# State carries by sync-engine transfers, four diagonal states, a root by logarithm and exponential with a Heron step, and a third norm row on GpSimd, in a fused scan-and-quantized-matmul kernel

## The reference

```python
def _s6(x, A_log, D, x_proj_w, dt_proj_w, dt_proj_b):      # x is layernorm(x)
    A = -jnp.exp(A_log)                                    # (512, 16)
    xp = jnp.einsum('bld,ed->ble', x, x_proj_w)            # 96 columns: rank 64, B 16, C 16
    delta = softplus(xp[..., :64] @ dt_proj_w.T + dt_proj_b)
    deltaA = exp(delta * A); deltaB_u = delta * B * x      # both (b, l, 512, 16)
    h = deltaA_t * h + deltaB_u_t; y_t = sum_n h_n * C_tn  # scan over 2048 steps
    return y + x * D
def _xla_quantized_matmul(x2d, weight_q, weight_scale):    # x2d is layernorm of the first layer's output
    amax = jnp.max(jnp.abs(x2d), axis=-1, keepdims=True)
    x_scale = jnp.maximum(amax, 1e-6) / 127.0
    x_q = clip(round(x2d / x_scale), -128, 127)            # int8
    return (x_q @ weight_q.T) * x_scale * weight_scale     # + bias, + x
```

## Time and profile before

| | |
|---|---|
| median of 3 runs | 2841.26 us (2841.11 to 2842.9) |
| the profiled execution's own time | 2839.73 us |
| its span, first to last instruction | 2837.9 us |
| busy: TensorE (PE) | 2798.8 us, 99% |
| busy: GpSimd (POOL) | 2758.2 us, 97% |
| busy: VectorE (DVE) | 2714.1 us, 96% |
| busy: ScalarE (ACT) | 2708.3 us, 95% |
| granted TensorE clock, mean | 0.998 |
| bytes moved | 321.24 MB, mean 113 GB/s |

### The profile page before, as it was taken

The page is one execution under the profiler, slowest core; times in us unless marked ns, Lnnn a source line. Parts: engine busy times, 40 slices in busy tenths (PEclk is TensorE's granted clock), DMA queues, the critical chain, the costliest instruction groups (busy, mean ns, idle before and its releaser), DMA issues.

```text
span 2837.9 us, 59945 instructions
## 1 busy us (share of the span) xinstructions
PE 2798.8 (99%) x22838; PEld 2544.0 (90%) x22900; DVE 2714.1 (96%) x2765; ACT 2708.3 (95%) x4990; POOL 2758.2 (97%) x1072
## 2 busy tenths in 40 slices
PE   8999999999999999999999999999999999999997
PEld 6889899899999898998998998989989989989886
DVE  6999999999999999999999999999999999999995
ACT  7999999999999999999999999999999999999993
POOL 4899999999999999999999999999999999999997
PEclk9999999999999999999999999999999999999999
DMA  5234434444434444344444344443444443444434
GB/s 188 94 106 101 129 103 127 115 115 96 127 109 115 114 100 129 102 125 118 113 98 126 110 114 116 100 129 101 125 119 113 98 127 109 114 116 98 116 91 82
DMA packets 198369, 321.24 MB, mean 113 GB/s; under 512 B 93057, under 2 KB 93057, under 8 KB 181698
## 3 DMA queue, kind: packets, MB, share of 16 engines
q1 hardware_dynamic: 164242, 250.29, 26.6%
q0 software_dynamic: 33840, 67.11, 15.4%
HBM read 212.70 MB, written 104.66 MB: 112 GB/s over the span
## 4 chain that ended last, share of the span: by engine, by line
PE 45%; POOL 35%; issue 18%; DMA 1%; DVE 0%; SPq 0%; POOLq 0%; ACT 0%; DVEq 0%
POOL A L482 27%; PE Y L707 15%; PE PB L685 10%; PE PB L682 10%; POOL C L499 3%; PE PM L747 2%; PE PM L766 2%; PE Y L703 2%; PE PM L810 2%; POOL C L491 2%; PE PM L795 1%; POOL RO L453 1%; PE PM L775 1%; PE PM L737 1%; POOL XN L438 1%
## 5 line engine op out<-in xcount | busy, mean ns | idle before, releaser
L482 POOL TENSOR_TENSOR A<-A,CB 128x2048 f32<-128x2048 f32 x511 | 2361.3, 4754 | 13.1 <-ACT CAR L545 10.9
L836 DVE TENSOR_TENSOR_SCAN A<-A,CAR,PB 128x512 f32<-128x512 f32 x1536 | 1845.8, 1264 | 40.9 <-PE PB L682 26.9
L538 ACT ACTIVATE A<-DEL,an 128x512 f32<-128x512 f32 x2048 | 1354.3, 713 | 0.4
L707 PE MATMUL Y<-idf,A 128*128 128x128 f32 x8192 | 1123.5, 273 | 1.9 <-POOL A L482 1.9
L707 PEld LDWEIGHTS Y<-idf,A 128*128 128x128 f32 x8192 | 945.5, 141 | 71.5 <-issue 41.9
L560 ACT ACTIVATE DB<-XN,BC 128x512 f32<-128x512 f32 x1408 | 966.5, 713 | 4.4 <-DVE XN L866 4.4
L685 PE MATMUL PB<-idf,DB 128*128 128x128 f32 x5632 | 801.5, 273 | 10.2 <-ACT DB L560 5.7
L685 PEld LDWEIGHTS PB<-idf,DB 128*128 128x128 f32 x5632 | 652.1, 141 | 49.0 <-issue 28.8
L682 PEld LDWEIGHTS PB<-DG,XN 128*128 128x128 f32 x5120 | 612.0, 192 | 61.3 <-issue 49.7
L682 PE MATMUL PB<-DG,XN 128*128 128x128 f32 x5120 | 638.4, 276 | 3.9 <-DVE A L836 3.3
L836 DVE TENSOR_TENSOR_SCAN A<-A,PB 128x512 f32<-128x512 f32 x512 | 589.4, 1203 | 30.6 <-PE PB L682 20.0
(11 more groups left out here) (88 smaller groups left out, 1661.1 us busy)
## 6 DMA issues: line engine op xcount, KB each, us to landing
CB<-c_rows SPq DMA_DIRECT2D x128, 1024.0 KB, 6.3
DG<-b_diag SPq DMA_DIRECT2D x160, 256.0 KB, 2.8
out<-bib SPq DMA_DIRECT2D x32, 1024.0 KB, 5.2
out<-X POOLq DMA_DIRECT2D x32, 1024.0 KB, 9.7
X<-in_x SPq DMA_DIRECT2D x31, 1024.0 KB, 5.5
out<-C POOLq DMA_DIRECT2D x31, 1024.0 KB, 8.9
b_diag<-DG SPq DMA_DIRECT2D x2, 1280.0 KB, 10.9
b_diag<-BC SPq DMA_DIRECT2D x160, 2.0 KB, 5.5
```

What stands on the lines that cost most here:

```text
L482: gp.tensor_tensor(A[s % NA][:, :, :], A[s % NA][:, :, :], CB[:, s % (4 * NG), :].unsqueeze(1).broadcast_to([128, KB, L]), ALU.mult).then_ ...
L538: act.activation(A[s % NA][:, g, :], DEL[k % 2][:, g, :], ACT.Exp, scale=an[:, g, n:n + 1])\
L707: i = pe.matmul(Y[j][:, g * 128:(g + 1) * 128], A[s % NA][:, g, j * 128:(j + 1) * 128], idf[:, :], is_transpose=True, start=False, stop=(n ...
L836: dve.tensor_tensor_scan(A[s % NA][:, g, :], A[s % NA][:, g, :], PB[(4 * s + g) % NPB][:, :], init, ALU.mult, ALU.add).then_inc(s_scan, 1)
```

## The change

- `carry` moves from ScalarE to the sync engine: a transfer from A's last column to CAR, with a semaphore of its own for each state (`s_car[n]`). `times_c` and the next chunk's `scan` wait for it.
- Diagonal states are 2, 6, 10 and 14; the other twelve are scaled (`act_b` has 48 instructions per chunk where it had 44).
- NXP = 3: one norm row of a chunk on ScalarE, three on GpSimd.
- The power on GpSimd is replaced. ScalarE (`root`) takes the logarithm of the largest square v, and the exponential of half of it, r. VectorE (`inv`) takes 1/r. GpSimd (`ascale`) forms v (1/r) + r, which is twice the root after one Heron step; the constants in the scale are doubled to match.
- All three tables of places are new.

```diff
-    DIAG = (2, 5, 8, 11, 14)
-    SCALED = tuple(n for n in range(NS) if n not in DIAG)
+    ROWS = {2: 4, 6: 4, 10: 4, 14: 4}
+    DIAG = tuple(ROWS)
+    SCALED = tuple(n for n in range(NS) if ROWS.get(n, 0) < T)
+    BYACT = tuple((n, j) for n in SCALED for j in range(ROWS.get(n, 0), T))
-    NXP = 2
+    NXP = 3
-        s_car = sem("s_car")
+        s_car = [sem(f"s_car{n}") for n in range(NS)]
+        def carried(k):
+            return 16 * (k + 1 - (k + 1) // CPB)
@@ sync engine
+            def carry(k, n):
+                s = NS * k + n
+                if k % CPB != CPB - 1:
+                    sp.wait_ge(s_scan, 4 * (s + 1))
+                    sp.dma_start(CAR[:, n, :], A[s % NA][:, :, L - 1], allow_slow_non_contiguous=True)\
+                      .then_inc(s_car[n], 16)
@@ GpSimd, ascale
-                gp.wait_ge(s_am, p + (T if p == END else 1))
-                gp.tensor_tensor(RO[:, 1, :], PW[:, 1, :], halves[:, :], ALU.pow).then_inc(s_as, 1)
+                gp.wait_ge(s_ir, p + 1)
+                gp.tensor_tensor(PW[:, 3, :], PW[:, 1, :], RO[:, 3, :], ALU.mult).then_inc(s_qu, 1)
+                gp.wait_ge(s_qu, p + 1)
+                gp.tensor_tensor(RO[:, 1, :], PW[:, 3, :], RO[:, 2, :], ALU.add).then_inc(s_as, 1)
...
-                gp.tensor_scalar(AM[:, 1, :], AM[:, 0, :], 1e-6 * D, 1.0 / (127.0 * D), ALU.max, ALU.mult).then_inc(s_zm, 1)
+                gp.tensor_scalar(AM[:, 1, :], AM[:, 0, :], 2e-6 * D, 1.0 / (254.0 * D), ALU.max, ALU.mult).then_inc(s_zm, 1)
@@ GpSimd, times_c
-                    gp.wait_ge(s_car, car_done(s))
+                    gp.wait_ge(s_car[n], carried(k))
@@ ScalarE
-            def carry(k, n):
-                s = NS * k + n
-                if k % CPB != CPB - 1:
-                    act.wait_ge(s_scan, 4 * (s + 1))
-                    act.activation(CAR[:, n, :], A[s % NA][:, :, L - 1], ACT.Copy).then_inc(s_car, 1)
+            def root(p):
+                act.wait_ge(s_am, p + (T if p == END else 1))
+                if p >= 1:
+                    act.wait_ge(s_as, p)
+                act.activation(PW[:, 2, :], PW[:, 1, :], ACT.Ln, bias=eps[:, 1:2]).then_inc(s_la, 1)
+                act.wait_ge(s_la, p + 1)
+                act.activation(RO[:, 2, :], PW[:, 2, :], ACT.Exp, scale=0.5).then_inc(s_ro, 1)
@@ VectorE
-                        dve.wait_ge(s_car, car_done(s - NS))
+                        dve.wait_ge(s_car[n], carried(k - 1))
+            def inv(p):
+                dve.wait_ge(s_ro, p + 1)
+                if p >= 1:
+                    dve.wait_ge(s_qu, p)
+                dve.reciprocal(RO[:, 3, :], RO[:, 2, :]).then_inc(s_ir, 1)
```

More of the change, by code:

```diff
@@ L7 @@
 PLACES = {
[L8 to L18, removed]
@@ L27 @@
[L27 to L39, removed]
@@ L40 @@
[L40 to L47, removed]
@@ new lines @@
+        885, 894, 905, 928, 933),
+        "delta": (-328, -284, -235, -221),
+        "dl_t": (-309, -291, -263, -215),
+        "du": (-241, -233, -135, -119),
+        "gather": (1216, 1240, 1295, 1314),
+        "idle": (247, 276, 296, 679),
+        "inv": (1630,),
+        "last_q": (1001, 1470, 1786, 1918),
+        "load": (-1797,),
+        "load_c": (17, 237, 390, 949),
+        "load_g": (127, 354, 507, 642),
+        "log0": (-1390,),
+        "put_bias": (-2127,),
+        "q_mm": (2047, 2065, 2123, 2170),
@@ new lines @@
+        "q_t": (1836, 1871, 1973, 2015),
+        "qt_out": (1892, 1950, 2000, 2052),
+        "root": (1618,),
+        "rstd0": (-1110,),
+        "scale_a": (2122, 2154, 2179, 2296),
+        "scale_out": (1189, 1260, 1438, 1757),
+        "scale_p": (2225, 2238, 2250, 2286),
+        "scales": (1647,),
+        "scan": (-1, 2, 28, 41, 62, 72, 74, 75, 78, 101, 127, 130, 133, 138, 148, 158, 165, 284, 307, 322,
+        396, 398, 425, 453, 488, 502, 514, 514, 529, 532, 535, 556, 563, 585, 589, 603, 641, 645, 669, 670,
@@ new lines @@
+        "bc_out": (-1082,),
+        "carry": (-151, 177),
+        "d_t": (-2138, -1928, -1666, -1482),
+        "decay": (-688, -517, -457, -415, -386, -378, -364, -331, -197, -191, -175, -141),
+        "delta": (-1724, -1452, -1420, -1232),
+        "dl_t": (-640, -504, -380, -378),
+        "du": (-783, -752, -615, -539),
+        "load": (-2031,),
+        "load_c": (145, 298, 369, 943),
+        "load_g": (-2112, -1829, -1610, -1379),
+        "log0": (-3909,),
+        "rstd0": (-3420,),
@@ L103 @@
+        "xt_out": (-2832, -2622, -2520, -2330),
 }
 LAST = {
[L105 to L116 removed]
@@ L117 @@
-        "scale_a": (7012, 7591, 8525, 9023),
-        "scale_out": (5826, 5947, 5965, 6001),
-        "scale_p": (5883, 6694, 6705, 7190),
-        "scales": (4187,),
-        "square": (1842, 2068, 2360, 2650),
-        "step": (5380,),
-        "var1": (2968,),
+        "add_c": (10005,),
+        "add_x": (9337,),
+        "amax": (5373,),
+        "ascale": (6247,),
+        "centre": (7133, 8575, 8687, 8959),
+        "gather": (1437, 1738, 2111, 2287),
+        "idle": (6433, 6748, 6781, 6989),
@@ new lines @@
+        "inv": (6266,),
+        "last_q": (10558, 10580, 10676, 10719),
+        "put_bias": (8553,),
+        "q_mm": (9996, 10293, 10358, 10398),
+        "q_t": (9658, 9761, 9943, 10267),
+        "qt_out": (11073, 11449, 11735, 12504),
+        "root": (4507,),
+        "scale_a": (10713, 10933, 11105, 11118),
+        "scale_out": (12357, 12625, 12631, 12849),
+        "scale_p": (10622, 10919, 11150, 11852),
+        "scales": (6637,),
+        "square": (2683, 2837, 2855, 3147),
+        "step": (6286,),
@@ L124 @@
+        "var1": (3667,),
 }
```

154 lines of the change are left out of this document (68 added, 86 removed), and 16 rows, old and new, of the table PLACES.

## The result

| | before | after |
|---|---|---|
| median | 2841.19 us (4 runs) | 3030.78 us (4 runs, 3026.71 to 3041.98) |
| ratio | | 1.0674, 95% interval 1.0661 to 1.0687 |
| span of the profiled execution | 2837.9 us | 3040.3 us |
| granted TensorE clock, mean | 0.998 | 0.974 |
| TensorE busy | 2798.8 us | 2837.6 us |

Slower by 6.7%, where 0.6% faster was forecast: the prediction was wrong, and outside its range. The loss sits in particular laps. Counted from one out<-C issue of GpSimd to the next, the laps of the changed kernel in which only 4 carries are made last 86.8 to 86.9 us each, and those with 12 or 16 carries last 92.7 to 97.0 us, 95.3 as a mean of 22. Before, 28 of these 29 laps lie between 86.6 and 87.0, whether carries are made or not.

What follows compares the result with a forecast made beforehand. GpSimd and TensorE were taken to bound the kernel together; from 2839.7 us, 25.4 less for 31 laps, plus 6 for carries and 2 for start gave 2822.3, plus 1.5 to the median: 2824, range 2810 to 2850.

Steps and rivals of the forecast that it cites:

- The carries on the sync engine: Carries as 384 sync-engine transfers: 2.6 us each (2.1 landing, 0.5 semaphore and issue), hidden everywhere before GpSimd's C products.
- the leads: A state's scans end ahead of its C product by 5.5 us (state 0) up to 8 to 13.
- two near places: Sync engine: C load behind carry 12 (6.8 against 7.0 us), carry 15 behind loads; allowed 0.2 us per lap, 6 total.
- C: Rival: carries land late, GpSimd waits at states 0, 15, 12; about 1.6 us per carry lap, 2856 us; chance 0.20.
- D: Rival: engines too close, short waits passed on at the normed rows' transpose; 0.7 us a lap, 2840 us; chance 0.17.
- GpSimd's group: Scale group on GpSimd, two small instructions replacing the power: 1.12 us instead of 2.67, 1.55 less per lap.
- the third norm row: One more norm row on GpSimd: 0.73 us added per lap.
- 31 x 0.82 = 25.4 us: GpSimd's net saving of 0.82 us a lap (86.73 to 85.91), over 31 laps.
- I had +2: Start and ramp, from the new queue order: 2 us longer (ends -5 and +6).
- VectorE's reciprocal: One small reciprocal on VectorE, 157 ns; ready about 1.8 us ahead, so no cost.
- my 85.0 and 86.1: ScalarE's lap: 85.0 us by spacings (the value taken), 86.1 by busy time.
- 1.82 forecast: TensorE: one state from diagonal to scaled, four groups, 1.82 us less per lap, to about 84.8, all slack.

Runs made afterwards that it cites:

- experiment 1: Changed kernel with the four diagonal loads of a chunk (and the diagonals' store) issued much earlier on the sync engine: 2852.47 us, 1.0036 times before.
- experiment 5: experiment 1 with GpSimd issuing out<-X just ahead of state 6's product instead of just ahead of the small scale group: 2849.62 us, 1.0031 times before.
- experiment 6: experiment 5 with one norm row back on ScalarE (NXP = 2, two rows on GpSimd): 2843.8 us, 1.0009 times before.

## Why the prediction was wrong

**The step that failed: "The carries on the sync engine".** It asked three things of a carry: how long it takes, whether GpSimd's product waits for it, and which load of C stands behind it. The first was right, 2.0 us landing and 0.6 issue against 2.6 in the sum. The second was right as far as the order goes: the leads I had added up as 5.5 to 13 us are 6.3 to 14.0 in experiment 1, and past the first two laps GpSimd waits for no carry there. That 2.6 us "fits everywhere" was not the whole of it, though: a carry that takes 8 us comes in every such lap, and it fell by luck on a state with a lead of 11. The third was done by halves. I looked for C loads behind carries, found two near places and allowed 6 us; the loads of diagonals I only counted ("four per lap"). They are on the same list, three of them behind carries, and the reader of a diagonal is TensorE, which I had down as the engine with slack. The order of the change shows it, DG<-b_diag directly below CAR<-A. In place of an allowance of 6 us the runs show TensorE standing still some 3 us for a diagonal at states 6 and 10 of each carry lap, with a lower clock behind it. What it cost: of 202.4 us more span, 189.5 go with experiment 1's edit (3040.3 less 2850.8), 183.1 of them between the first and last out<-C and 6.4 ahead of it. No rival of mine had it; C looked at GpSimd at states 0, 12 and 15, D at the norm rows. GpSimd does wait 66.3 us for the load of C at state 12, the near place of the prediction, and for carries at state 15, but as a consequence: with the loads of diagonals early both are gone past the first two laps.

**A term mis-sized: GpSimd's group.** Put at 1.12 us, it measures 1.97 as a mean of 29 laps of experiment 1, where before it was 2.63; so the saving is 0.66 a lap, not 1.55, and the third norm row costs 0.83. Net 0.17 longer by these two, where 0.82 shorter was forecast; the 29 laps are 86.95 as a mean in experiment 1, 86.70 before, and the other 0.08 is spread over the rest. The power's 2.15 us before held about 1 us of what out<-C and out<-X had left (the product ahead of it overlaps it by 1.08 in one lap), product between them or not, and I booked it all as the power. The new group inherits the same 1 us. GpSimd's busy time, which was to fall by 25 us, rose from 2758.2 to 2761.3. The 31 x 0.82 = 25.4 us are thus none: from first to last out<-C experiment 1 takes 2597.2 us, before 2590.4. With 5.4 at the start (I had +2) and 0.6 at the end this is experiment 1's 12.9 us over the kernel before. Rival D's place is seen as well, TensorE waiting for three norm rows (L755, "issue": 31.4 us, 29 times, in experiment 5), but nothing holds GpSimd up there.

**Right:** the carry's own duration; the leads; VectorE's reciprocal ahead of GpSimd (it is late only in the stalled laps); ScalarE, 85.4 in experiment 1 between my 85.0 and 86.1 (the lap of 84.08 that I took as one without carries holds three, 0.2 us each). TensorE lost about what was forecast by the groups (L682 638.4 us before, L700 515.0 in experiment 1, and the plain transposes' 801.5 became 868.9: 1.75 a lap, 1.82 forecast), but its busy time per lap fell by 1.0 only, from 86.6 to 85.6, probably as short gaps between groups lie under the records and count as busy.

The best version here is experiment 6 at 2843.8 us: not better than the kernel before (1.0009, 1.0000 to 1.0018). Four engines of 84.8 to 86.0 us in a lap of 86.7 left little to be had from relieving one of them.

## What to carry to other kernels

When an instruction that waits is put on a queue that works in order, list everything behind it on that queue up to the next such wait, and for each item its reader and how early it must land; not just the item you have in mind. A load that depends on nothing late belongs ahead of such waits, and here one place ahead for each of three loads was worth 153 us. A small instruction's spacing in a timeline may contain the rest of what went before it: before booking it as its own cost, look for one of the same kind elsewhere in the lap.

## What was new about the hardware

- On GpSimd the issue of a transfer lets the next instruction start after 0.86 us, but about 0.5 us more stay behind, unseen in overlapping records. Two transfers ahead of the group of small instructions made its first one take 1.18 us instead of 0.28, and the group 1.97 instead of 1.05 (medians, experiment 5 against the run with the transfer behind the group). Where GpSimd waits for something else in between, it costs nothing.
- A transfer of 512 pieces of 4 bytes lands in 2.0 us when alone, and in 7.9 to 9.4 when issued 0.6 to 1.2 us behind the start of a megabyte from GpSimd's queue (8.0 behind three megabytes in its own queue, of which the last was issued 3.4 us ahead of it). Issued 0.0 to 0.6 us behind the start of GpSimd's out<-X it lands ahead of it, in 2.0 to 3.2.
- After TensorE has stood 2.8 us, its clock in the 10 us in which it starts again is 0.83 of full as a mean, and 24 matmuls take 4.14 us instead of 2.84. TensorE was busy 71 us more in the changed kernel for the same products; how much of the 189.5 us of span came by that was not isolated.
